# Attention with a feed-forward layer woven in: feed-forward pieces moved one group ahead, behind the sums of the single key tile

## The chip, the cores and the metric

The kernel runs on one core of one Trainium2 chip. TensorE (PE in the profile) does the matmuls, ScalarE (ACT) the sigmoids, VectorE (DVE) the elementwise work, GpSimd (POOL) a few additions, and SyncE (SP) issues the transfers. The metric is the device time of one execution in microseconds (us). A difference of 0.2% of it, about 9 us, is what a measurement of this kernel can tell from no change.

## The reference

The reference is one transformer layer with the normalisation behind each half. `x` has 2 sequences of 4,096 tokens, 256 wide; attention has 16 heads of 16. Each score passes a sharp sigmoid of its own instead of a softmax, so a query has no normalising sum over the keys:

```
x_norm = layernorm(x, gamma, beta)
q, k = l2_normalize(heads(x_norm @ w_q)), l2_normalize(heads(x_norm @ w_k))
v = heads(x @ w_v)
resonance = 0.5 + 0.5 * tanh((q @ k.T - 0.27) * 15)        # per head, all 4096 x 4096
gate_q, gate_k = 0.25 + 0.75 * sigmoid(q @ g_q), 0.25 + 0.75 * sigmoid(k @ g_k)
fused = (resonance * gate_q[:, None] * gate_k[None, :]) @ v
x = layernorm(x + fused @ w_o + b_o)
h = silu(fp4_linear(x, w_gate)) * fp4_linear(x, w_up)      # 704 wide
out = layernorm(x + fp4_linear(h, w_down))
```

`fp4_linear` rounds both operands, in blocks of 16, to a 4-bit grid and multiplies them in float32.

## The kernel before

A first phase makes q, k, the gates and the gated v and puts them in HBM. The second phase, which is nearly the whole time, is attention in 64 **units**. A unit is 512 queries of one group of four heads against all 32 key tiles of 128. It has 128 score blocks of 128 keys by 512 queries, one PSUM bank each, cut into 44 **groups**: `GROUPS = [4, 2] * 20 + [2, 2, 2, 2]`. The groups of four use banks 0 to 3, the groups of two banks 4 and 5, in turn, so while ACT takes the sigmoid of one group PE can fill only the other's banks.

The order is written out by hand. ACT takes the groups in order (line 660). PE goes through **steps**: at step n it waits until ACT has finished group n, writes the scores of group n+2 (line 1203) into the banks that group n has just left, then adds the finished key tiles to the unit's sums (line 1213), as `sums_at(n)` says:

```
at[4 * c] = [3 * c - 1, 3 * c]                    # two key tiles
at[4 * c + 2] = [0, 1] if c == 0 else [3 * c + 1] # a single key tile
```

So four steps repeat: a step n = 4c writes four scores and sums two key tiles, 4c+1 writes two scores, 4c+2 writes four scores and sums a single key tile, and 4c+3 writes two scores. These four steps are called a **period** here.

From the second sequence block on, a unit also carries the output projection and feed-forward of one tile of 128 tokens, in ten **pieces** of PE work. They go through the one PSUM bank 6, and each waits until DVE or ACT has emptied the bank behind the piece before. The pieces are H0, H1 (transposes, lines 1249 and 1253), D0, D1 (the down projection in two halves, line 1263; the four belong to the tile of the unit before), P (output projection, line 1225, from the tile `m_f` that a transfer brings), X (transposes, line 1231) and G0 to G3 (gate and up projection, line 1240). The tables `BEGIN` and `END` say at which step a piece runs; `GATE_ACT` says behind which of its groups ACT takes the sigmoid of G0 and of G1 (line 665). The four lines that set it, in the unit of PE:

```
for kt in sums_at(n):
    ...
    sums(kt, par, g)
if n in END and ends(j, g):
    end_piece(END[n], u - HG - 1)
if n in BEGIN and begins(j, g):
    begin_piece(BEGIN[n], u - HG)
```

and in the unit of ACT, behind the activation of group n:

```
if n in GATE_ACT and begins(j, g):
    k, p = u - HG, GATE_ACT[n]
    act.wait_ge(l_G, 4 * k + p + 1)
    act.activation(m_sg[:, p * FH:(p + 1) * FH], ps[:, C_BANK, 0:FH], ACT.Sigmoid)\
```

The first four units carry no pieces of a tile; 60 units do. The last four tiles go through a short tail phase.

Of the kernel before, what the change touches and what calls it, by code (L numbers as in the profile page):

```python
# [13 lines left out]
P = 128  # L14
# [60 lines left out]
FH = F // 2  # L75


BEGIN = {7: "P", 19: "X", 23: "G0", 27: "G1", 31: "G2", 35: "G3"}
END = {0: "H0", 3: "H1", 11: "D0", 15: "D1"}
GATE_ACT = {25: 0, 29: 1}  # L80
PREP = {3 + 4 * i: i for i in range(9)}
NTAIL = HG
LOOP_FROM = 2
# [37 lines left out]
def build(nc, x, w_q, w_k, w_v, g_q, g_k, w_o, b_o, gamma, beta, w_gate, w_up, w_down, out):  # L121
# [12 lines left out]
    with ExitStack() as ctx:  # L134
# [222 lines left out]
        def units(fori, unit, before=lambda r: None):  # L357


            for j in range(LOOP_FROM):  # L360
                for g in range(HG):
                    unit(j, g)
            with fori(LOOP_FROM, NUNIT // HG) as j:
                before(j - LOOP_FROM)
                for g in range(HG):
                    unit(j, g)

        def begins(j, g):

            return not isinstance(j, int) or j >= 1  # L370

        def ends(j, g):

            return not isinstance(j, int) or HG * j + g > HG
# [224 lines left out]
        def _(act):  # L599
# [55 lines left out]
            def unit(j, g):  # L655
                u = HG * j + g
                for n in range(NGRP):
# [3 lines left out]
                                   scale=2 * SHARP / QK_UP ** 2, bias=-2 * SHARP * THRESH).then_inc(b_act, 1)  # L661
# [3 lines that stand above are left out]
# [449 lines left out]
        def _(pe):  # L1114
# [92 lines left out]
            def sums(kt, par, g):  # L1207

                for h in range(HG):
                    n = kt * HG + h  # L1210
                    q = max(i for i in range(NGRP) if FIRST[i] <= n)
                    r = res[:, (NGRP // 2 * g + q // 2) % RES_CYCS, BANK[q % 2] + n - FIRST[q], :]
                    ins = pe.matmul(ps[32 * h:32 * h + 32, SUM_BANK, :], vt[:, par, n * HD:n * HD + 32], r,  # L1213
                                    start=kt == 0, stop=kt == KT - 1, skip_group_check=True)
                ins.then_inc(b_pv, 1)
# [3 lines left out]
            def begin_piece(what, k):  # L1219

                if what == "P":
                    pe.wait_ge(l_f, 16 * (k + 1))
                    wait(pe, l_hT, 2 * k)
                    for c in range(DC):
                        ins = pe.matmul(c_ps[:, 0:D], m_f[:, c, :], wo[:, c, :], start=c == 0, stop=c == DC - 1)  # L1225
                    ins.then_inc(l_P, 1)
                elif what == "X":
                    pe.wait_ge(l_xq, k + 1)
                    wait(pe, l_fin, k)
                    for c in range(DC):  # L1230
                        ins = pe.transpose(c_ps[:, c * P:(c + 1) * P], m_xq[:, c * P:(c + 1) * P], idf[:, :])
                    ins.then_inc(l_X, 1)
                else:
                    p = int(what[1])
                    if p == 0:
                        pe.wait_ge(l_xT, k + 1)
                    else:
                        pe.wait_ge(l_ge, 4 * k + p)
                    for c in range(DC):
                        ins = pe.matmul(c_ps[:, 0:FH], m_xqT[:, c, :], wguT[:, c, p * FH:(p + 1) * FH],  # L1240
                                        start=c == 0, stop=c == DC - 1)
                    ins.then_inc(l_G, 1)

            def end_piece(what, k):

                if what == "H0":
                    pe.wait_ge(l_hq, k + 1)
                    for j in range(4):
                        ins = pe.transpose(c_ps[:, j * P:(j + 1) * P], m_hq[:, j * P:(j + 1) * P], idf[:, :])
                    ins.then_inc(l_H, 1)  # L1250
                elif what == "H1":
                    pe.wait_ge(l_hT, 2 * k + 1)
                    pe.transpose(c_ps[:, 0:P], m_hq[:, 4 * P:5 * P], idf[:, :])
                    pe.transpose(ps[0:FR, C_BANK, P:2 * P], m_hq[:, 5 * P:F], idf[:, :]).then_inc(l_H, 1)  # L1254
                else:
                    half = int(what[1])
                    if half == 0:
                        pe.wait_ge(l_hT, 2 * k + 2)

                        pe.wait_ge(l_r, k + 1 if isinstance(k, int) and k == NT - NTAIL - 1 else k + 2)  # L1260
                    for j in range(3 * half, 3 * half + 3):
                        w = P if j < FT_FULL else FR
                        ins = pe.matmul(c_ps[:, 0:D], m_hqT[0:w, j, :], wdnT[0:w, j, :],  # L1263
                                        start=j == 0, stop=j == FT_FULL)
                    if half == 1:
                        ins.then_inc(l_D, 1)
# [20 lines left out]
            def unit(j, g):  # L1287
                u, par = HG * j + g, g % 2
                for n in range(NGRP):
# [7 lines left out]
                    for kt in sums_at(n):  # L1297
                        if kt == 0:
                            pe.wait_ge(b_ev, u + 1)
# [5 lines that stand above are left out]
                    if n in PREP and isinstance(j, int) and j == 0 and g == 2:  # L1305
# [8 lines left out]
            units(pe.Fori, unit)  # L1314
            for n in END:
                end_piece(END[n], NT - NTAIL - 1)

# [70 lines left out]
```

## Time and profile before

| | |
|---|---|
| median of 3 runs | 4472.55 us (4470.05 to 4476.02) |
| the profiled execution's own time | 4469.53 us |
| its span, first to last instruction | 4467.7 us |
| mean granted TensorE clock | 0.985 of full speed |
| busy PE / ACT / DVE | 93% / 90% / 35% of the span |
| chain that ended last, by engine | PE 68%, ACT 16% |

The share of a busy engine is an average. What a moved piece is worth is read from the order of time in one unit: which engine waits for which at each step.

### The profile page before, as it was taken

The page shows a single profiled execution, that of the slowest core. Times are in us where ns is not written, and L with a number is a line of the kernel's source. Part 1 is how long each engine was busy: PE and PEld are TensorE (multiplying, and loading weights), DVE is VectorE, ACT ScalarE, POOL GpSimd, SP SyncE. Part 2 cuts the span into 40 slices and gives each one's busy share as a digit, 9 for nine tenths or more (in the row PEclk, how much of TensorE's full clock was granted, in tenths as well). Part 3 has the DMA queues.
Part 4 walks back from the last instruction along what each step waited for, and adds up shares of the span by engine and source line. Part 5 has one row for each costly group of instructions (what it writes and reads, how often), then busy time and mean ns, then how long its engine had stood idle before and what let it go on. Part 6 is the DMA issues. An engine that isn't in the chain of part 4 may idle for free.

```text
span 4467.7 us, 80907 instructions
## 1 busy us (share of the span) xinstructions
PE 4139.1 (93%) x28776; PEld 1293.7 (29%) x28776; DVE 1558.9 (35%) x4536; ACT 4026.8 (90%) x3275; POOL 159.2 (4%) x120
## 2 busy tenths in 40 slices
PE   7977889999999999999999999999999999999997
PEld 5651222222222222222222222222222222222223
DVE  6772013233333323332333332333233333333235
ACT  4658999999999999999999999999999999999993
POOL 2330000000000000000000000000000000000001
PEclk9989999999999999999999999999999999999998
DMA  3445433443344434443344334433444344434440
GB/s 110 125 116 83 61 61 61 76 76 60 57 75 77 64 61 67 77 67 62 63 77 70 61 62 77 77 60 61 72 77 64 63 66 76 72 57 64 77 80 14
DMA packets 180059, 315.51 MB, mean 71 GB/s; under 512 B 65265, under 2 KB 141809, under 8 KB 154609
## 3 DMA queue, kind: packets, MB, share of 16 engines
q1 hardware_dynamic: 179568, 309.41, 41.2%
q8 instruction: 255, 4.18, 0.4%
q14 instruction: 236, 1.93, 0.2%
HBM read 266.82 MB, written 42.47 MB: 69 GB/s over the span
## 4 chain that ended last, share of the span: by engine, by line
PE 68%; ACT 16%; issue 8%; DVE 4%; DMA 2%; SPq 2%; POOL 0%; ACTq 0%; POOLq 0%; DVEq 0%
PE ps L1213 34%; PE ps L1203 19%; ACT room L660 15%; PE ps L1240 7%; PE ps L1263 4%; DMA m_f<-fused_t 1%; DVE room L807 1%; SPq L486 1%; PE ps L1158 0%; SPq L462 0%; DVE st L761 0%; DMA vt<-v_gated 0%; DVE xnT L797 0%; PE ps L1225 0%; PE ps L1169 0%
## 5 line engine op out<-in xcount | busy, mean ns | idle before, releaser
L660 ACT ACTIVATE room<-ps 128x1024 f32<-128x1024 f32 (+1 forms) x2816 | 3792.9, 1416 | 246.2 <-PE ps L1203 231.7
L1213 PE MATMUL ps<-room,vt 128*32 128x512 f32 x16384 | 2064.4, 605 | 0.0
L1203 PE MATMUL ps<-qs,room 64*128 64x512 f16 x8198 | 1330.5, 384 | 249.5 <-ACT room L660 214.3
L1203 PEld LDWEIGHTS ps<-qs,room 64*128 64x128 f16 x8198 | 311.2, 93 | 1802.3 <-ACT room L660 1133.9
L1213 PEld LDWEIGHTS ps<-room,vt 128*32 128x32 f32 x16384 | 389.7, 109 | 954.8 <-issue 954.8
L1240 PE MATMUL ps<-wguT,m_xqT 128*128 128x352 f32 x960 | 348.2, 485 | 0.0
L905 DVE TENSOR_TENSOR vz<-ps,vz 128x352 f32<-128x352 f32 x120 | 63.0, 525 | 757.7 <-ACT vz L665 757.7
L910 DVE TENSOR_TENSOR vz<-ps,vz 128x352 f32<-128x352 f32 x120 | 63.0, 525 | 595.9 <-PE ps L1240 595.9
L1263 PE MATMUL ps<-wdnT,wqk 128*128 128x256 f32 x720 | 198.9, 404 | 0.6 <-DVE wqk L875 0.6
L1240 PEld LDWEIGHTS ps<-wguT,m_xqT 128*128 128x128 f32 x960 | 162.6, 189 | 105.2 <-issue 54.3
L561 POOL TENSOR_TENSOR m_x<-m_x,bo 128x256 f32<-128x256 f32 x60 | 43.6, 727 | 3972.7 <-DMA m_x<-in_L_attn_x_dram 3972.7
L920 DVE TENSOR_TENSOR fs<-ps,gqb 128x512 f32<-128x512 f32 x64 | 44.3, 692 | 315.1 <-PE ps L1213 315.1
L1263 PEld LDWEIGHTS ps<-wdnT,wqk 128*128 128x128 f32 x720 | 121.8, 188 | 56.8 <-issue 46.6
L892 DVE TENSOR_TENSOR m_x<-ps,m_x 128x256 f32<-128x256 f32 x60 | 25.5, 425 | 319.5 <-PE ps L1225 319.5
L1150 PE MATMUL ps<-wqk,xnT 128*128 128x512 f32 x256 | 125.4, 612 | 6.8 <-DVE xnT L797 6.8
L881 DVE TENSOR_TENSOR wv<-ps,m_x 128x256 f32<-128x256 f32 x60 | 25.5, 425 | 291.2 <-PE ps L1263 291.2
L619 ACT COPY room<-ps 128x512 f32<-128x512 f32 x64 | 37.4, 584 | 75.1 <-PE ps L1158 40.7
L874 DVE COPY wqk<-ps 128x128 f32<-128x128 f32 x60 | 17.5, 292 | 242.3 <-PE ps L1254 242.3
L1225 PE MATMUL ps<-wo,m_f 128*128 128x256 f32 x240 | 67.8, 405 | 8.9 <-DMA m_f<-fused_t 8.9
L1158 PE MATMUL ps<-wv,xT 128*128 128x256 f32 x256 | 72.0, 404 | 0.0
L553 POOL TENSOR_TENSOR room<-room 128x2048 f16<-128x2048 f32 x16 | 65.4, 4085 | 0.2 <-PE ps L1131 0.2
L723 DVE TENSOR_TENSOR m_ln<-m_ln 128x1 f32<-128x1 f32 x360 | 57.4, 159 | 19.3 <-DVE m_ln L722 8.3
(165 smaller groups left out, 2211.0 us busy)
## 6 DMA issues: line engine op xcount, KB each, us to landing
room<-k_parts SPq DMA_DIRECT2D x520, 256.0 KB, 9.8
vt<-v_gated SPq DMA_DIRECT2D x65, 1024.0 KB, 17.5
qs<-q_parts SPq DMA_DIRECT2D x520, 32.0 KB, 10.4
gqb<-q_gates SPq DMA_DIRECT2D x256, 64.0 KB, 2.1
room<-in_L_attn_x_dram SPq DMA_DIRECT2D x16, 512.0 KB, 4.2
v_gated<-vz SPq DMA_DIRECT2D x64, 128.0 KB, 2.1
q_parts<-room SPq DMA_DIRECT2D x32, 256.0 KB, 2.1
k_parts<-room SPq DMA_DIRECT2D x32, 256.0 KB, 2.2
```

The source lines that it names most:

```text
L553: pool.tensor_tensor(part[1], qk[:, par], part[0], ALU.subtract).then_inc(a_lo, 1)
L660: act.activation(res[:, c, o:o + m, :], ps[:, o:o + m, :], ACT.Sigmoid, scale=2 * SHARP / QK_UP ** 2, bias=-2 * SHARP * THRESH).then_inc(b ...
L723: after(dve.tensor_tensor(t, t, ha, ALU.mult))
L905: dve.tensor_tensor(m_tg[:, cols], ps[:, C_BANK, 0:FH], m_sg[:, cols], ALU.mult)\
L910: dve.tensor_tensor(m_hb[:, cols], ps[:, C_BANK, 0:FH], m_tg[:, cols], ALU.mult)\
L1150: pe.matmul(ps[:, 4 + t % 2, :], xnT[:, c, tok], wqk[:, c, :], start=c == 0, stop=c == DC - 1)
L1158: ins = pe.matmul(ps[:, 6, 0:D], xT[:, c, tok], wv[:, c, :], start=c == 0, stop=c == DC - 1)
L1203: ins = pe.matmul(ps[:, BANK[n % 2] + i, :], ks[o:o + HROWS, par, h // 2, kt * P:(kt + 1) * P], qs[o:o + HROWS, par, h // 2, :], start=Tru ...
L1213: ins = pe.matmul(ps[32 * h:32 * h + 32, SUM_BANK, :], vt[:, par, n * HD:n * HD + 32], r, start=kt == 0, stop=kt == KT - 1, skip_group_che ...
L1225: ins = pe.matmul(c_ps[:, 0:D], m_f[:, c, :], wo[:, c, :], start=c == 0, stop=c == DC - 1)
L1240: ins = pe.matmul(c_ps[:, 0:FH], m_xqT[:, c, :], wguT[:, c, p * FH:(p + 1) * FH], start=c == 0, stop=c == DC - 1)
L1263: ins = pe.matmul(c_ps[:, 0:D], m_hqT[0:w, j, :], wdnT[0:w, j, :], start=j == 0, stop=j == FT_FULL)
```

## The change

Eight of the ten pieces move one step ahead. H0 and H1 stay. The two sigmoids of ACT move ahead by one group with G0 and G1. Nothing is added or removed.

```diff
-BEGIN = {7: "P", 19: "X", 23: "G0", 27: "G1", 31: "G2", 35: "G3"}
-END = {0: "H0", 3: "H1", 11: "D0", 15: "D1"}
-GATE_ACT = {25: 0, 29: 1}
+BEGIN = {6: "P", 18: "X", 22: "G0", 26: "G1", 30: "G2", 34: "G3"}
+END = {0: "H0", 3: "H1", 10: "D0", 14: "D1"}
+GATE_ACT = {24: 0, 28: 1}
```

On PE, one period with a piece of line 1240 in a unit looked like this before (matmuls in program order; L1203 are scores, L1213 sums, x6 is a step's two scores and the next step's four):

```order
 L1203 MATMUL ps<-qs,room 128x512 x6
 L1213 MATMUL ps<-room,vt 32x512 x4
 L1203 MATMUL ps<-qs,room 128x512 x2
 L1240 MATMUL ps<-wguT,m_xqT 128x352 x2
 L1203 MATMUL ps<-qs,room 128x512 x4
 L1213 MATMUL ps<-room,vt 32x512 x8
```

and at the same place it looks like this now:

```order
 L1203 MATMUL ps<-qs,room 128x512 x6
 L1213 MATMUL ps<-room,vt 32x512 x4
 L1240 MATMUL ps<-wguT,m_xqT 128x352 x2
 L1203 MATMUL ps<-qs,room 128x512 x6
 L1213 MATMUL ps<-room,vt 32x512 x8
```

The two scores that stood ahead of the piece stand behind it, together with the next four.

On ACT, the difference around the two sigmoids (L665) among the groups of four banks (128x2048) and of two (128x1024):

```order
-L660 ACTIVATE room<-ps 128x1024
-L665 ACTIVATE vz<-ps 128x352
-L660 ACTIVATE room<-ps 128x2048
-L660 ACTIVATE room<-ps 128x1024
+L665 ACTIVATE vz<-ps 128x352
+L660 ACTIVATE room<-ps 128x1024
+L660 ACTIVATE room<-ps 128x2048
+L660 ACTIVATE room<-ps 128x1024
```

Each sigmoid now stands ahead of the group of two that it stood behind.

## Rows read from the trace of the kernel before

**Rows 1.** The page: busy time of the engines.

```profile
PE 4139.1 (93%) x28776; PEld 1293.7 (29%) x28776; DVE 1558.9 (35%) x4536; ACT 4026.8 (90%) x3275; POOL 159.2 (4%) x120
```

**Rows 2.** Timeline, period with G0: start us, duration us, engine, line, [idle before <-releaser].

```profile
3531.97 1.06 PE L1213 MATMUL ps<-room,vt 128*32 128x512 f32 x8
3532.97 0.39 PE L1203 MATMUL ps<-qs,room 64*128 64x512 f16 x2
3533.28 0.89 PEld L1240 LDWEIGHTS ps<-wguT,m_xqT 128*128 128x128 f32 x4 [0.23 <-issue]
3533.28 1.45 PE L1240 MATMUL ps<-wguT,m_xqT 128*128 128x352 f32 x4
3534.67 0.61 PE L1203 MATMUL ps<-qs,room 64*128 64x512 f16 x4
3535.15 0.48 ACT L665 ACTIVATE vz<-ps 128x352 f32<-128x352 f32 x1
3535.20 1.92 PE L1213 MATMUL ps<-room,vt 128*32 128x512 f32 x16
3535.49 4.79 ACT L660 ACTIVATE room<-ps 128x2048 f32<-128x2048 f32 x3
3537.06 1.00 PE L1203 MATMUL ps<-qs,room 64*128 64x512 f16 x6
3537.99 1.07 PE L1213 MATMUL ps<-room,vt 128*32 128x512 f32 x8
```

**Rows 3.** Timeline, a period of an early unit, where only short transposes are woven in.

```profile
492.08 5.48 ACT L660 ACTIVATE room<-ps 128x1024 f32<-128x1024 f32 x4 [0.19 <-PE ps L1203]
492.48 1.07 PE L1213 MATMUL ps<-room,vt 128*32 128x512 f32 x8
...
494.93 0.60 PE L1203 MATMUL ps<-qs,room 64*128 64x512 f16 x4 [0.47 <-ACT room L660]
...
497.32 0.90 PE L1203 MATMUL ps<-qs,room 64*128 64x512 f16 x6
...
497.75 2.79 ACT L660 ACTIVATE room<-ps 128x1024 f32<-128x1024 f32 x2 [0.19 <-PE ps L1203]
498.15 1.07 PE L1213 MATMUL ps<-room,vt 128*32 128x512 f32 x8
```

**Rows 4.** Timeline, the other periods of the unit of rows 2.

```profile
3508.47 1.06 PE L1213 MATMUL ps<-room,vt 128*32 128x512 f32 x8
...
3515.53 1.56 PE L1263 MATMUL ps<-wdnT,wqk 128*128 128x256 f32 x6
3517.03 0.60 PE L1203 MATMUL ps<-qs,room 64*128 64x512 f16 x4
...
3521.49 1.54 PE L1263 MATMUL ps<-wdnT,wqk 128*128 128x256 f32 x5
...
3523.61 1.93 PE L1213 MATMUL ps<-room,vt 128*32 128x512 f32 x16
...
3527.54 0.44 PE L1231 MATMUL ps<-idf,m_xq 128*128 128x128 f32 x2
...
3555.29 6.54 ACT L660 ACTIVATE room<-ps 128x1024 f32<-128x1024 f32 x6 [0.30 <-PE ps L1203]
3555.39 1.07 PE L1213 MATMUL ps<-room,vt 128*32 128x512 f32 x8
```

**Rows 5.** Waits from 600 to 4370 us: waiter <- releaser, total us, times, longest.

```profile
ACT room L660 <- PE ps L1203: 192.9, 641, 2.2
PE ps L1225 <- DMA m_f<-fused_t: 8.9, 12, 1.9
```

**Rows 6.** Timeline, piece P in a unit whose transfer came late.

```profile
917.86 1.13 PE L1225 MATMUL ps<-wo,m_f 128*128 128x256 f32 x4 [1.88 <-DMA m_f<-fused_t]
918.91 0.61 PE L1203 MATMUL ps<-qs,room 64*128 64x512 f16 x4
```

**Rows 7.** Windows, an early unit: span, busy PE, PEld, DVE, ACT, POOL (instructions), PEclk.

```profile
470.00:530.10 60.10, 53.85 (x416) 14.03 (x410) 7.09 (x17) 57.97 (x45) 0.00 (x0) 1.00 0.41 64
```

## The prediction

> **What bounds the kernel now.** I read the busy shares first. PE is busy for 93% of the span and ACT for 90% [rows 1], so neither is plainly the bound, and the answer lies in how they hand groups to each other. The waits say that ACT stood idle for scores 641 times, 192.9 us in all, in the stretch that carries the pieces [rows 5]. The order of time inside a unit then shows two kinds of period.
>
> In a period without a heavy piece the two engines chase each other. Follow [rows 3] as a loop: four scores start at 494.93, two key tiles' sums stand behind them (0.53 later, and 1.86 long, by the same steps in [rows 2]), the two scores start at 497.32, ACT starts on them at 497.75, which is 0.43 behind their start. From the start of a group of two on ACT to the four scores that wait for the group of four behind it are 2.85 us (492.08 to 494.93), which holds both activations and the handover. 0.53 + 1.86 + 0.43 + 2.85 = 5.67 us, and the period from 492.48 to 498.15 is 5.67 us. PE waits in it (0.47 us at 494.93); its work does not fill it. So a loop through both engines, not a busy share, sets the time there, and such sums hit the rows to 0.01 us.
>
> In a period with a heavy piece PE works without a pause. [Rows 2], start to start: sums of the single tile 1.00, two scores 0.31, G0 1.39, four scores 0.53, two tiles' sums 1.86, six scores 0.93. That is 6.02 us, the whole period. The piece stands behind the two scores, so ACT has these early, and what it delays are the next four scores, and ACT has a group of four and then one of two to work on before it needs them. The eight periods from the sums of step 6 to those of step 38 take 46.92 us in this unit (3508.47 to 3555.39, [rows 4]).
>
> **What the move does to the loop.** A piece at step 4c+2 stands between the single tile's sums and the two scores of step 4c+3. No group is left to cover them: while PE does this step, ACT takes one group of two and one of four, and the next group of two needs exactly those two scores. ACT's two groups take 2.67 us from start to start (half of the 5.34 worked out below), 2.81 to the end of the second with the 0.14 of overlap given there; the 2.85 above leave 0.04 for the handover. From the end of group 4c+2 PE so needs 0.04 to start, 0.53 for four scores, 1.00 for the sums, the piece, and 0.43 until ACT can begin. With G's 1.39 these are 3.39, so ACT, free after 2.67, stands for 0.72 us. The lateness is not absorbed, since the next step of this kind waits for the group of four behind that late group of two. This closes a new loop, from sums to sums: 1.00 + piece + 0.43 + 2.85 + 0.53 = 4.81 us + the piece.
>
> By periods, each piece's length being its row less the 0.06 to 0.07 us by which a successor starts before a modelled end (1.45 against 1.39 for G0, [rows 2]):
> - P: 1.05 [rows 6], loop 5.86.
> - D0: 1.50 (3515.53 to 3517.03, [rows 4]), 6.31.
> - D1: its rows run into the scores; between 1.21, when the first score starts, and 1.59, from its start to the sums at 3523.61 less 0.53. I take 1.50, as D0 [rows 4]: 6.31.
> - X: 0.37 [rows 4]. The loop would be 5.18, less than ACT needs for four groups: 5.48 [rows 3] less 0.14 by which neighbours on ACT overlap (3535.15 + 0.48 against 3535.49, [rows 2]), 5.34. So 5.34.
> - G0, G1: 1.39. ACT's sigmoid now stands ahead of the late group of two. It can start when G has ended, 0.07 behind the start of the two scores, and delays the group by 0.34 (3535.15 to 3535.49, [rows 2]); 0.41 and a handover, instead of 0.43. Handover between nothing and 0.1: I take 0.04, 6.22 each.
> - G2: 6.20. G3: 5.98, since the scores of step 38 are two instead of four (0.31 for 0.53).
>
> Sum 48.44 against 46.92: 1.52 us more. One wait goes: at 3555.29 ACT stood 0.30 us for its scores, 0.44 with the overlap of 0.14 that was lost too [rows 4]. PE, which now waits for ACT at each single-tile step, has those scores written in time, and nothing behind step 38 has a piece. Net 1.08 us a unit, 65 us over 60 units.
>
> P also moves towards the transfer that it needs. It waited for `m_f` 12 times, 8.9 us in all [rows 5]; it now comes 0.31 us earlier in its unit, and there was some slack of 0.2 us behind it that the new loop has not. 12 times 0.5 us is 6 us; a few units in which it landed just in time will wait too. I take 9 us, from bounds of 0 (the longer unit lets the queue catch up) and 32 (0.53 us in all 60).
>
> The other waits of the moved pieces keep their distances of four steps, with periods that are longer, so DVE's work between them stays covered: D1 to X, say, with 0.42 us of DVE needed by X and four steps between. SP's and POOL's orders are unchanged. PE works in the same order of pieces, so nothing in bank 6 is overtaken.
>
> One cost no row shows: a piece whose weights are loaded right behind the sums. [Rows 2] bound it from both sides. Behind sums a score starts 1.00 after them, before their modelled end of 1.06, with its own weight load at the same instant; behind scores the piece starts 0.08 before their end. Both changes cost alike, so I take zero, and plus or minus 0.1 us for the seven heavy pieces, 42 us over all, for the range. PE also saves where six scores run together (0.93 with a wait inside, against 0.31 + 0.53), but it waits in this loop, so this buys nothing.
>
> 65 + 9 = 74 us on the profiled execution's 4469.5 us gives 4543.5; the median of the runs shown is 3 us above it, so I predict **4547 us**, 1.7% slower.
>
> The Trainium skill, TensorE: Matmul & The Clock Gate (Part 2, the step on LDWEIGHTS), states that PE pulls a weight load ahead of running matmuls when row groups don't conflict or the background buffer is free. The trace does not agree at these seams: the load of G0's weights starts with its first matmul, both at 3533.28 [rows 2]. By that rule a piece's first load would vanish under the sums, which is the second rival's case.
>
> **The rivals.**
> 1. *PE's work alone sets the period (faster).* If the two scores were not missed by ACT, the period would be PE's sum with six scores at 0.31 + 0.43 instead of 0.31 + 0.53 + part of a wait: 0.1 to 0.2 us less than 6.02 for seven pieces in 60 units, 42 to 84 us, some 4410 us. For it: PE is unbroken now [rows 2]. Against it: the loop of 4.81 + piece uses only distances that the rows show. It decides at the piece's length: below about 1.0 us (5.8 to 5.9 less 4.81) the new place is no worse, above it is; P is near that, D and G are beyond.
> 2. *Loads hide under the sums (no change).* The weight rows of G0 have 0.89 us for four, 0.22 each. If the first of each heavy piece ran under the sums, seven times 0.2 us, 1.4 us a unit, would go, and 1.08 + 0.15 (the transfer) becomes -0.17, 10 us over 60 units: about 4462 us, and within 0.2% of now up to 4481. Against it: no first load in rows 2 runs ahead.
> 3. *The transfer binds every unit (slower still).* If `m_f` were late in all 60 units by the present mean of 8.9 / 12 = 0.74 us and the 0.5, P would cost 74 us instead of 9: some 4615 us. Against it: 48 of 60 do not wait now.
>
> PE's clock is no rival: an early unit has PE busy for 53.85 of 60.10 us at a granted clock of 1.00, the higher level of 2.4 GHz [rows 7], more idle than the new loop brings.
>
> **How the numbers follow.** The new loop 0.82, PE's work alone 0.05, hidden loads 0.06, the transfer 0.07. The forecast's own bounds are 42 us for the seam each way and 20 us for transfer and handover, seldom together. The range 4505 to 4600 holds most of the 0.82 and leaves out the rivals. Faster by over 0.2% 0.06, within 0.2% 0.05, slower 0.89.
>
> **What will show it.** A unit of 63.5 us or so where it was 62.4; seven groups of two on ACT per unit that wait some 0.6 us for the scores behind a piece; PE waiting for ACT ahead of the four scores, 0.2 us or so, in the periods with D and G; periods of 6.2 to 6.3 us there, and 5.3 to 5.4 at X. I am wrong if the groups behind a piece don't wait, or if a piece behind sums starts much later or earlier than 1.00 us after them.

## The result, and the profile after

The changed kernel takes 4556.23 us (median of 4 runs, 4546.6 to 4561.25) against 4473.52 us for the kernel before beside it (4 runs): 1.0183 times the time, 95% interval 1.0164 to 1.0202, so 82.7 us or 1.8% slower. The prediction was 4547 us. The profiled execution took 4546.6 us, its span 4544.8.

The page, busy time of the engines after the change:

```profile
PE 4145.1 (91%) x28776; PEld 1290.8 (28%) x28776; DVE 1558.4 (34%) x4536; ACT 4009.3 (88%) x3275; POOL 159.2 (4%) x120
```

Against [rows 1] both busy engines lost share, and the numbers of their instructions are unchanged. The chain that ended last says where the time is now, by engine:

```profile
PE 46%; ACT 33%; issue 13%; DVE 4%; DMA 2%; SPq 1%; ACTq 0%; POOL 0%; POOLq 0%; DVEq 0%
```

It was 68% PE and 16% ACT. PE alone no longer carries the chain; it goes back and forth between the two engines, as in a loop. The waits of the changed kernel from 600 to 4445 us:

```profile
ACT room L660 <- PE ps L1203: 264.3, 454, 1.9
PE ps L1203 <- ACT room L660: 234.4, 563, 2.0
ACT vz L665 <- PE ps L1240: 23.3, 60, 0.4
PE ps L1225 <- DMA m_f<-fused_t: 8.5, 12, 1.8
```

ACT's waits for scores are fewer and longer than in [rows 5] (454 against 641, 264.3 us against 192.9), a sigmoid waits for its piece 60 times, once a unit, and P's waits for its transfer are about what they were. PE's waits for ACT grew as well; the kernel before had, from 600 to 4370 us:

```profile
PE ps L1203 <- ACT room L660: 173.1, 235, 2.2
```

The timeline of one unit shows the loop itself. G2's period and the sums that begin G3's (PE, its weight loads PEld, and ACT):

```profile
3344.34 0.61 PE L1203 MATMUL ps<-qs,room 64*128 64x512 f16 x4 [0.31 <-ACT room L660]
3344.88 1.07 PE L1213 MATMUL ps<-room,vt 128*32 128x512 f32 x8
3345.87 0.89 PEld L1240 LDWEIGHTS ps<-wguT,m_xqT 128*128 128x128 f32 x4 [0.84 <-issue]
3345.87 1.45 PE L1240 MATMUL ps<-wguT,m_xqT 128*128 128x352 f32 x4
...
3347.26 0.82 PE L1203 MATMUL ps<-qs,room 64*128 64x512 f16 x6
3347.69 5.48 ACT L660 ACTIVATE room<-ps 128x1024 f32<-128x1024 f32 x4 [0.71 <-PE ps L1203]
...
3350.53 0.61 PE L1203 MATMUL ps<-qs,room 64*128 64x512 f16 x4 [0.28 <-ACT room L660]
3351.07 1.06 PE L1213 MATMUL ps<-room,vt 128*32 128x512 f32 x8
```

Read it as the prediction's sum: sums to piece 0.99, piece to scores 1.39, scores to ACT 0.43, ACT's group of two to the four scores behind its group of four 2.84 (3347.69 to 3350.53), scores to sums 0.54; 6.19 us from sums to sums, 6.20 forecast. The row of ACT starts with the group of two that waited 0.71 us for the scores behind the piece, and PE waits 0.28 to 0.31 us at each end. In [rows 2] no wait is marked on the rows of the period; a small one is hidden in PE's six scores, whose row takes 1.00 us there and 0.82 here.

The eight periods of this unit, by the start of the single tile's sums at steps 6, 10, 14, 18, 22, 26 and 38, and at step 6 of the next unit (the sums at steps 30 and 34 are the two above), with the rows of ACT that start with a late group of two:

```profile
3308.48 1.06 PE L1213 MATMUL ps<-room,vt 128*32 128x512 f32 x8
...
3314.35 1.06 PE L1213 MATMUL ps<-room,vt 128*32 128x512 f32 x8
...
3317.28 5.48 ACT L660 ACTIVATE room<-ps 128x1024 f32<-128x1024 f32 x4 [0.65 <-PE ps L1203]
...
3320.66 1.06 PE L1213 MATMUL ps<-room,vt 128*32 128x512 f32 x8
...
3323.67 8.17 ACT L660 ACTIVATE room<-ps 128x1024 f32<-128x1024 f32 x6 [0.92 <-PE ps L1203]
...
3327.05 1.07 PE L1213 MATMUL ps<-room,vt 128*32 128x512 f32 x8
...
3332.43 1.06 PE L1213 MATMUL ps<-room,vt 128*32 128x512 f32 x8
...
3338.65 1.06 PE L1213 MATMUL ps<-room,vt 128*32 128x512 f32 x8
...
3353.88 14.65 ACT L660 ACTIVATE room<-ps 128x1024 f32<-128x1024 f32 x12 [0.72 <-PE ps L1203]
...
3357.05 1.07 PE L1213 MATMUL ps<-room,vt 128*32 128x512 f32 x8
...
3372.12 1.07 PE L1213 MATMUL ps<-room,vt 128*32 128x512 f32 x8
```

P 5.87, D0 6.31, D1 6.39, X 5.38, G0 6.22, G1 6.23, G2 6.19, G3 5.98: together 48.57 us where [rows 4] had 46.92. From step 6 to step 6 the unit takes 63.64 us; the unit of [rows 4] took 62.32, its next sums of step 6 starting, in the trace of before, at

```profile
3570.79 1.07 PE L1213 MATMUL ps<-room,vt 128*32 128x512 f32 x8
```

So 1.32 us a unit; over 60 units 79 us of the 82.7, and the rest is less than the runs can tell.

### The profile page after: what moved, and what is told of

Same layout as the page of the kernel before. It is cut to its first block, busy times and chain, and to the rows that moved or that the text cites. A ratio compares the mean times of both kernels' runs of the same rounds, so it can differ in the third digit from the quotient of the medians.

```text
span 4544.8 us, 80907 instructions
## 1 busy us (share of the span) xinstructions
PE 4145.1 (91%) x28776; PEld 1290.8 (28%) x28776; DVE 1558.4 (34%) x4536; ACT 4009.3 (88%) x3275; POOL 159.2 (4%) x120
## 4 chain that ended last, share of the span: by engine, by line
PE 46%; ACT 33%; issue 13%; DVE 4%; DMA 2%; SPq 1%; ACTq 0%; POOL 0%; POOLq 0%; DVEq 0%
ACT room L660 32%; PE ps L1213 19%; PE ps L1203 13%; PE ps L1240 7%; PE ps L1263 4%; DMA m_f<-fused_t 1%; DVE room L807 1%; SPq L486 1%; SPq L462 0%; PE ps L1158 0%; DVE st L761 0%; DMA vt<-v_gated 0%; DVE xnT L797 0%; ACTq L659 0%; PE ps L1169 0%
## 5 line engine op out<-in xcount | busy, mean ns | idle before, releaser
L1213 PE MATMUL ps<-room,vt 128*32 128x512 f32 x16384 | 2059.9, 603 | 0.0
L1203 PE MATMUL ps<-qs,room 64*128 64x512 f16 x8198 | 1325.6, 383 | 317.2 <-ACT room L660 275.7
L1203 PEld LDWEIGHTS ps<-qs,room 64*128 64x128 f16 x8198 | 313.4, 94 | 1590.9 <-ACT room L660 864.5
L1213 PEld LDWEIGHTS ps<-room,vt 128*32 128x32 f32 x16384 | 389.3, 109 | 951.0 <-issue 951.0
L665 ACT ACTIVATE vz<-ps 128x352 f32<-128x352 f32 x120 | 55.6, 463 | 28.6 <-PE ps L1240 23.3
```

Source lines behind the costliest of these rows:

```text
L1203: ins = pe.matmul(ps[:, BANK[n % 2] + i, :], ks[o:o + HROWS, par, h // 2, kt * P:(kt + 1) * P], qs[o:o + HROWS, par, h // 2, :], start=Tru ...
```

## The experiments

All edit the three tables or one piece of the kernel before. e1_light, e2_gates, e3_down and e5_halves ran on one chip, with the kernel before at 4464.29 us, the other four on one with it at 4462.39; both are below the 4473 us that most of the expectations set out from, so differences to before are compared, not times. With intervals of 0.1 to 0.2% to each side a difference of 4 to 9 us can be told.

**P and X alone** (e1_light).

```diff
-BEGIN = {7: "P", 19: "X", 23: "G0", 27: "G1", 31: "G2", 35: "G3"}
+BEGIN = {6: "P", 18: "X", 23: "G0", 27: "G1", 31: "G2", 35: "G3"}
```

> Only the two short pieces are moved, P to step 6 and X to step 18; D and G stay behind the groups of two. Theory (the piece delays the two scores behind it, and the loop 4.81 us + piece decides): P's loop is 5.86 us where its period was 5.75, X's 5.18 is below ACT's own 5.34, so a unit grows by 0 to 0.11 us and the time by 0 to 9 us with the transfer of m_f: 4473 to 4482 us, no change that can be told. Rival (each piece behind sums pays a seam of 0.1 to 0.2 us whatever its length): 0.2 to 0.4 us a unit, 4485 to 4497 us.

4473.85 us against 4464.29: 1.0019 (1.001 to 1.0028), 9.6 us more. That is just over the theory's upper end of 9 us, so it can be told after all, and it is below the seam rival's 12 to 24. Between the starts of ACT's groups 6 and 10, P's period, are 5.89 us where before had 5.74 by the same measure; X's is 5.75 as before. The transfer did not add to it; from 600 to 4370 us P waited for it less than in [rows 5]:

```profile
PE ps L1225 <- DMA m_f<-fused_t: 2.8, 7, 0.9
```

**G0 to G3 alone** (e2_gates).

```diff
-BEGIN = {7: "P", 19: "X", 23: "G0", 27: "G1", 31: "G2", 35: "G3"}
-GATE_ACT = {25: 0, 29: 1}
+BEGIN = {7: "P", 19: "X", 22: "G0", 26: "G1", 30: "G2", 34: "G3"}
+GATE_ACT = {24: 0, 28: 1}
```

> Only G0 to G3 and their two sigmoids are moved. Theory: periods of 6.2 to 6.3 us for G0 to G3 where they were 6.02, 5.93, 5.85 and 5.85, less 0.44 us behind G3: 0.5 to 0.9 us a unit, 4505 to 4527 us. Rival (P's nearer transfer or the order as a whole makes the loss): below 4485 us.

4515.53 us, 1.0121 (1.0106 to 1.0137): 51 us more, inside the theory's 32 to 54 over before (its 5.85 for G3's old period is by ACT's groups; by the sums it was 5.62, which puts the theory's middle at 45). It is most of the loss, with P, X, D0, D1 and the transfer left alone.

**D0 and D1 alone** (e3_down).

```diff
-END = {0: "H0", 3: "H1", 11: "D0", 15: "D1"}
+END = {0: "H0", 3: "H1", 10: "D0", 14: "D1"}
```

> Only D0 and D1 are moved. Theory: periods of 6.3 and 6.4 us where they were 5.95 and 6.05, 0.7 us a unit, of which the X period behind them gives back up to 0.5 us because ACT finds its scores ready there: 0.2 to 0.4 us a unit, 4485 to 4497 us. Rival (nothing is given back): 0.7 us a unit, 4515 us.

4482.32 us, 1.0039 (1.0025 to 1.0052): 18 us more, the theory's 12 to 24; the rival wanted 42. The timeline around D0, D1 and X, the single tile's sums of steps 10, 14, 18 and 22, and the two late groups on ACT:

```profile
3268.10 1.06 PE L1213 MATMUL ps<-room,vt 128*32 128x512 f32 x8
...
3271.02 5.48 ACT L660 ACTIVATE room<-ps 128x1024 f32<-128x1024 f32 x4 [0.53 <-PE ps L1203]
...
3274.41 1.07 PE L1213 MATMUL ps<-room,vt 128*32 128x512 f32 x8
...
3277.42 8.16 ACT L660 ACTIVATE room<-ps 128x1024 f32<-128x1024 f32 x6 [0.92 <-PE ps L1203]
...
3280.80 1.06 PE L1213 MATMUL ps<-room,vt 128*32 128x512 f32 x8
...
3286.18 1.07 PE L1213 MATMUL ps<-room,vt 128*32 128x512 f32 x8
```

6.31 and 6.39 us for D0 and D1, and then 5.38 for X where it had 5.75: behind D1, ACT takes six groups in one go (8.16 us), because PE, which had waited, is ahead with its scores. A period paced by ACT gives back 0.37 us of what two late periods took. The three parts add up: 9.6 + 51 + 18 = 79 us, against 82.7 for all together.

**The sigmoids left behind** (e4_sigmoid): all pieces as changed, `GATE_ACT` as before.

```diff
 BEGIN = {6: "P", 18: "X", 22: "G0", 26: "G1", 30: "G2", 34: "G3"}
 END = {0: "H0", 3: "H1", 10: "D0", 14: "D1"}
-GATE_ACT = {24: 0, 28: 1}
+GATE_ACT = {25: 0, 29: 1}
```

> All eight pieces moved as in the change, but the sigmoids of G0 and G1 stay behind groups 25 and 29. Theory: the late group of two is started 0.41 us behind the scores without them, but then 0.34 us of sigmoid stand between it and the group of four behind it, for which the next step waits: loops of 4.81 + 1.39 + 0.34 = 6.54 us where they are 6.26 and 6.22, 0.6 us a unit, 36 us above the changed kernel, 2.6% above before. Rival (the sigmoids' new wait for PE, 23 us in the changed kernel, is part of the loss): 20 to 30 us below the changed kernel.

4581.96 us, 1.0275 (1.0259 to 1.0291): 120 us above before, 37 more than the change's 82.7, as the theory said. So moving the sigmoids along did not cause the loss; it spares 37 us. The group of two behind G0 and what follows on ACT:

```profile
3361.14 1.02 ACT L660 ACTIVATE room<-ps 128x1024 f32<-128x1024 f32 x1 [0.42 <-PE ps L1203]
...
3362.06 0.46 ACT L665 ACTIVATE vz<-ps 128x352 f32<-128x352 f32 x1
3362.40 4.57 ACT L660 ACTIVATE room<-ps 128x2048 f32<-128x2048 f32 x3
...
3364.34 0.60 PE L1203 MATMUL ps<-qs,room 64*128 64x512 f16 x4 [0.64 <-ACT room L660]
```

The sigmoid now stands inside the late stretch, between the group of two and the group of four (0.34 us), and PE waits 0.64 us ahead of its four scores. Ahead of the late group, as in the change, the same 0.34 us run while ACT would wait for the scores anyway.

**Half of G** (e5_halves): the first of G's two accumulating matmuls behind the single tile's sums, the second where it was.

```diff
-BEGIN = {7: "P", 19: "X", 23: "G0", 27: "G1", 31: "G2", 35: "G3"}
+BEGIN = {7: "P", 19: "X", 22: "G0", 26: "G1", 30: "G2", 34: "G3"}
+REST = {23: 0, 27: 1, 31: 2, 35: 3}
...
-                    for c in range(DC):
+                    for c in (0,):
...
+                    if n in REST and begins(j, g):
+                        rest(REST[n])
```

> G0 to G3 are cut into their two accumulating matmuls: the first half, 0.70 us, runs behind the single tile's sums, the second behind the two scores as before; all else is as before. Theory: 4.81 + 0.70 = 5.51 us is below the 5.8 to 6.0 us that PE's work takes, so the new place costs nothing: 4464 to 4482 us. Rival (the place behind sums costs by itself, a seam of 0.1 to 0.2 us each): 4497 to 4521 us. Rival (cost goes with the work moved): half of what moving G0 to G3 whole costs, 4490 to 4500 us.

4496.43 us, 1.008 (1.0066 to 1.0093): 32 us more. The theory's figure is missed; by the total alone the rival of half the moved work holds (4490 to 4500 us), and the seam rival's lower end is less than 1 us away. The timeline says what it is: the single tile's sums of steps 22, 26, 30, 34 and 38, and in full the G1 period (the numbers of lines are one higher in this kernel):

```profile
3296.84 1.06 PE L1214 MATMUL ps<-room,vt 128*32 128x512 f32 x8
...
3302.89 1.07 PE L1214 MATMUL ps<-room,vt 128*32 128x512 f32 x8
3303.88 0.30 PEld L1241 LDWEIGHTS ps<-wguT,m_xqT 128*128 128x128 f32 x2 [0.84 <-issue]
3303.88 0.86 PE L1241 MATMUL ps<-wguT,m_xqT 128*128 128x352 f32 x2
...
3304.67 0.39 PE L1204 MATMUL ps<-qs,room 64*128 64x512 f16 x2
3304.99 0.30 PEld L1246 LDWEIGHTS ps<-wguT,m_xqT 128*128 128x128 f32 x2 [0.23 <-issue]
3304.99 0.86 PE L1246 MATMUL ps<-wguT,m_xqT 128*128 128x352 f32 x2
3305.78 0.11 PEld L1204 LDWEIGHTS ps<-qs,room 64*128 64x128 f16 x4 [0.49 <-ACT room L661]
...
3308.99 1.06 PE L1214 MATMUL ps<-room,vt 128*32 128x512 f32 x8
...
3315.04 1.07 PE L1214 MATMUL ps<-room,vt 128*32 128x512 f32 x8
...
3320.86 1.06 PE L1214 MATMUL ps<-room,vt 128*32 128x512 f32 x8
```

Each half takes 0.79 us from start to start, behind the sums (3303.88 to 3304.67) and behind the scores (3304.99 to 3305.78) alike, so 1.58 for both where the whole piece takes 1.39. Each half shows a weight load that starts with its first matmul. That is 0.19 us more of PE's own work a piece; the seam behind the sums is 0.99 us, where [rows 2] have 1.00. The four periods are 6.05, 6.10, 6.05 and 5.82 us. Before, with the sums of steps 22, 26 and 38 in [rows 2] and [rows 4] and those of steps 30 and 34 at

```profile
3543.92 1.06 PE L1213 MATMUL ps<-room,vt 128*32 128x512 f32 x8
...
3549.77 1.06 PE L1213 MATMUL ps<-room,vt 128*32 128x512 f32 x8
```

they were 6.02, 5.93, 5.85 and 5.62. So G1 to G3 grew by 0.17 to 0.20 us each, as by the cut, and G0 by 0.03, since PE's work did not quite fill its period: together 0.6 us a unit, 36 us, where the run took 32. The cut accounts for the time, and nothing is left for the place; but the run's total alone could not show this. The next pair can.

**A short G at both places** (e7_short_old, e8_short_new). Both leave out G's second matmul; the second kernel also has the tables of e2_gates.

```diff
-                    for c in range(DC):
+                    for c in (0,):
...
-                                        start=c == 0, stop=c == DC - 1)
+                                        start=True, stop=True)
```

> Leaves out the second of the two accumulating matmuls of G0 to G3, half of the gate and up contraction; the places are those of before. A short G took 0.79 us from start to start in the run with halves. Theory: PE's work of a G period falls from 5.84 to 5.24 us and the 5.67 us loop through both engines takes over: 0.15 to 0.35 us less in each of four periods, 36 to 84 us below the kernel before.

> The same short G0 to G3 as in the run beside it, but behind the single tile's sums, with the sigmoids moved along. Theory (the move costs only what a piece exceeds 0.9 to 1.0 us): 4.81 + 0.79 = 5.60 us is below the 5.67 us loop, so the time is that of the short pieces at the old place, within 10 us. Rival (standing behind the sums costs by itself): slower than that by half of what moving whole G0 to G3 cost, 20 to 30 us. Rival (a seam cost per piece): slower by 0.1 to 0.2 us for each of 240 pieces, 24 to 48 us.

4439.65 us (0.9948 of before, 0.9934 to 0.9961) at the old place and 4434.83 us (0.9942, 0.9929 to 0.9956) behind the sums: 5 us apart, within both intervals. The move that costs 51 us with pieces of 1.39 us costs nothing that can be told with pieces of 0.79. The late groups are gone too: behind the sums, ACT takes 18 groups from behind G1's sigmoid on without a marked wait.

```profile
3256.92 23.33 ACT L660 ACTIVATE room<-ps 128x1024 f32<-128x1024 f32 x18
```

The gain of both against before, 23 and 28 us, fell short of the expected 36 to 84 us. A unit did get shorter by 0.9 us in both traces (61.47 us between the first groups of neighbouring units, against 62.39), 55 us over 60 units; part of it was lost at the turns of the loop, below.

**One step later still** (e6_two_tiles): the pieces behind the sums of two key tiles.

```diff
+BEGIN = {8: "P", 20: "X", 24: "G0", 28: "G1", 32: "G2", 36: "G3"}
+END = {0: "H0", 3: "H1", 12: "D0", 16: "D1"}
+GATE_ACT = {26: 0, 30: 1}
```

> The eight pieces are put one step behind the old places, behind the sums of two key tiles; the sigmoids one group later too. Theory: the loop then holds 1.86 us of sums instead of 1.00, 5.67 us + piece: 6.72 for P, 7.17 and 7.26 for D0 and D1, 6.04 for X, 7.06 for each G, 55.4 us for the eight periods instead of 46.92: 8.5 us a unit, 510 us, some 4975 us on a chip where before takes 4464. Rival (any place behind sums costs the same seam or lost cover): as the changed kernel, 80 us above before.

4954.68 us, 1.1102 (1.1082 to 1.1123): 492 us more, against 510 by the loop. The two late groups of two on ACT behind G2 and behind G3:

```profile
3638.40 5.48 ACT L660 ACTIVATE room<-ps 128x1024 f32<-128x1024 f32 x4 [1.57 <-PE ps L1203]
...
3645.45 1.02 ACT L660 ACTIVATE room<-ps 128x1024 f32<-128x1024 f32 x1 [1.57 <-PE ps L1203]
```

They are 7.05 us apart; 5.67 + 1.39 makes 7.06. The same eight pieces cost six times as much where each period's sums ahead of them are 0.86 us longer.

## Why the prediction was right

- **The loop.** Right, and but for D1 term by term: the periods came out at 5.87, 6.31, 6.39, 5.38, 6.22, 6.23, 6.19 and 5.98 us, against 5.86, 6.31, 6.31, 5.34, 6.22, 6.22, 6.20 and 5.98. Shown by the rows, by the short pieces that don't cost, and by the longer sums that cost 492 us.
- **D1** was mis-sized by 0.08 us: the upper of its two bounds, 1.59, was the right one; 5 us over 60 units.
- **The wait that goes behind G3** was forecast at 0.44 us a unit. From step 38 to the next step 6 the units took 15.40 us before (3555.39 to 3570.79) and 15.07 after: 0.33, so 7 us too much was taken off. Together with D1 and smaller terms, the 1.08 us a unit was 1.32.
- **PE without a pause** in the heavy periods was not quite so. In G0's period, [rows 2], PE's six scores hold a wait of 0.18 us (1.00 us against 0.82 back to back), and with half of G0's matmuls left out at the old place the period is still 6.03 us (sums at 3251.99 and 3258.02). No term hung on it, since the old periods were read from the rows.
- **The transfer of P** was forecast at 9 us. The 12 waits of 8.9 us became 12 of 8.5. Moving P and X alone cost 9.6 us, of which P's longer period, 0.12 us by the sums (5.87 against 5.75) and 0.15 by the groups' starts, is 7 to 9, and P waited for its transfer for 2.8 us there. So this term was nearly nothing. Added by mistake, it made up for part of the 14 us by which the units were forecast too short (0.24 us in each of 60), and the total of 74 us came near the measured 82.7 partly for that reason.
- **The seam.** Zero was right: 0.99 us from sums to piece, where 1.00 was taken.
- **The signs.** A unit of 63.64 us for 63.5, PE's waits of 0.28 to 0.31 for 0.2, and 5.38 at X came as named. The seven groups of two that wait some 0.6 us did not: four wait in the unit shown, behind D0, D1, G2 and G3, for 0.65 to 0.92 us. Behind G1 it is the sigmoid that waits (23.3 us in 60 times), and behind P and G0 the profile marks no wait.
- **PE's work alone (faster)** is refuted: PE waits at each of these steps. The crossover named there, a piece of about 1.0 us, is borne out from both sides: P, at 1.05, costs 0.12 to 0.15 us, and the short G, at 0.79, nothing.
- **Loads under the sums** is refuted: behind the sums the piece's first load again starts with its first matmul (3345.87).
- **The transfer in every unit** is refuted: 12 waits as before.

## What to carry to other kernels

Filler work between two engines that hand buffers to each other belongs behind the handover that the other engine will need next, not ahead of it. Add up the loop, from one engine's release back to its next one, with the filler inside: as long as it stays below the time that a period takes anyway the place is free, and each further tenth of a microsecond is lost nearly in full, less what a following period paced by the other engine gives back (0.37 us behind D1 here). Cutting the filler to fit was no free remedy here, since each cut cost 0.19 us of PE's time.

## What the runs showed of the hardware

The two kernels with the short G gained less than their units. Two things happened at the turn of the loop, where every fourth unit begins. The first is a second pause of PE. In the traces of before and after PE waits there for ACT ahead of H0, 1.6 to 2.2 us; with the short G it then stops once more, in the middle of the transposes of H0, behind nothing that the profile shows ("issue"). For the short G at the old place, the waits from 600 to 4370 us and one turn:

```profile
PE ps L1249 <- issue: 25.5, 13, 2.5
```

```profile
1084.69 0.61 PE L1203 MATMUL ps<-qs,room 64*128 64x512 f16 x4 [1.84 <-ACT room L660]
...
1087.45 0.69 PE L1249 MATMUL ps<-idf,xh 128*128 128x128 f32 x2 [1.78 <-issue]
```

Behind the sums the short G has the same pause 13 times, 27.5 us; the kernel before and the changed one never have it. The second thing is the granted clock, which stands at half, the level of 1.2 GHz, in windows at the turn. With the short G at the old place this came 13 times between 600 and 4350 us, 71.7 us in all, in the trace of before 8 times, 44.4 us. The first of each, windows with PEclk in the third column from the end (the short G, then before):

```profile
1086.70:1093.50 6.80, 6.05 (x26) 1.27 (x26) 0.69 (x1) 3.31 (x3) 0.72 (x1) 0.50 0.70 144
```

```profile
1098.00:1104.80 6.80, 5.81 (x26) 1.06 (x24) 0.61 (x1) 4.35 (x4) 0.72 (x1) 0.50 0.54 124
```

Half of the additional 27.3 us, some 14 us by this estimate, is work that would have been done at the full clock. The 13 turns at which the clock fell are those with the second pause, but at three of them it fell before that pause began (at 3848.0 us, for one, against 3849.8), and in the trace of before it fell at 8 turns that have no second pause. So it is not shown that the second pause lowers the clock, and why PE stops there was not tried. In the waits within the units, 0.3 us each in the changed kernel, the clock did not fall: that trace has six such stretches between 600 and 4445 us, all where a fourth unit begins.
